# A windowed-attention transformer on one core: the scores split in two halves with a turn and a projection between them, and the output product moved to another PSUM bank

## The chip, the cores and the metric

One core of one Trainium2 chip runs the whole program. The time is the device time of one execution in microseconds (us). A kernel's figure is the median of several executions. Smaller is better.

## The reference, cut to what matters

The input x is 4 sequences of 512 tokens with 128 channels. First comes one RWKV time-mixing layer, then a transformer of 6 layers. This is the part of a layer that the change touches:

```python
def attn_layer(x, Wqkv, qs, ksc, Wo):          # x: (4, 512, 128), tokens shifted before
    q, k, v = split(x @ Wqkv, 3)               # 16 heads of 64
    q, k = l2norm(q) * qs, l2norm(k) * ksc     # then rotary tables on both
    ...
    # windows of 32 tokens; each looks at itself and the window before
    sim  = einsum('bhwie,bhwje->bhwij', bq, bk2) * 8.0
    sim  = where(mask, -max, sim)
    attn = softmax(sim, -1)
    out  = einsum('bhwij,bhwje->bhwie', attn, bv2)
    return out @ Wo                            # + x
# behind it: centre, normalise, x @ W1 + b1, a * gelu(gate), @ W2 + b2, + x
```

## The kernel before, in words

The function `time_mixing` does the RWKV layer in about the first 120 us of the profile. All that follows is `transformer`. Its work is cut into items, one for each layer and sequence (6 x 4 = 24), and each item into four blocks of 128 tokens, numbered t = 0 to 3. That makes 96 blocks. One step of the main loop handles several blocks at different ages: it projects block `step`, scores block `step - 2` and finishes block `step - 3`. Each engine has a program of its own written out by hand, in which the order of the calls is the order of execution. An engine waits only at a semaphore, and everything queued behind the waiting instruction waits with it.

In one step PE (TensorE) does the following, in this order (L1380 to L1415):

- `project` V0, Q0 and Q1: each is three matmuls of 128x512 (L1202 to L1204) into bank 0 or bank 1. Between them stand `turn_qk` of chunk 0 and, by t, the feed-forward pieces `expand` j=2 (t=1) and `centre` (t=3).
- at t=0, `widen_rstd` (L1341), which waits for `rooted`, the end of DVE's reciprocal square root (L922).
- `weigh(step-3, 1)`: the second half of probabilities times v, 64 small matmuls (L1284) into the two banks of the tensor `wide`. Of each bank's 512 columns, the first 4 x 65 = 260 are used.
- `turn_o(step-3, 0)`: four transposes (L1299) into bank 2. They wait for `o_normed`.
- `score(step-2)`: two mask matmuls (L1236), then 64 calls of small matmuls into banks 4 and 5. The trace counts each call as two matmuls and two weight loads (L1246 x12288 over 96 blocks, so 128 of each a block). Only the last call for each bank raises `scored`.
- `turn_o(step-3, 1)`, `project` K0, `project` K1, `turn_qk(step-1, 3)`.
- `merge_heads(step-3)`: the output product, 16 matmuls (L1313) into bank 4, columns 0 to 127. Since bank 4 also holds the scores, it waits until DVE's first `shift` has read them (`shifted[0]`).
- at t=1 `contract` (L1368), then `turn_probs` for r=0 and r=1 (L1264), each waiting for the exponential of its half. Then by t: `expand` j=0 (t=0), `turn_out` (t=2, last layer only), `variance` (t=3, L1332).
- `project` V1, which waits for `squared[2]`, then `turn_qk(step-1, 2)`, `weigh(step-2, 0)`, `turn_qk(step-1, 1)`, and at t=0 `expand` j=1, which waits for `hidden_ready`, DVE's gate (L984).

DVE (VectorE), in its order (L998 to L1027): `root`, `rotate` 0 (L879, L885), `normalise(step-3, 1)` (L946, L949), `rotate` 1, `maximum` 0 and 1 (L928, both wait for `scored`), `shift` 0 (L936), `sum_squares` 0 (L895), `shift` 1, `rotate` 2, `residual` (L959, reads the output product), `sum_squares` 1, `rotate` 3, and then `sum_squares` 2 and 3 and `normalise(step-2, 0)`, with `scale_xn`, `gate`, `take_var` and `finish_item` put in by t.

ACT (ScalarE), in its order (L1143 to L1178): `take_v`, `take_qk` 0 and 1, `square` 0 (L1064), `take_o` 0, `square` 1, `take_o` 1, `exponentiate` 0 (L1080), `take_qk` 3, `exponentiate` 1, at t=0 `shift_tokens`, `square` 2, `take_probs` 0 and 1 (L1087), at t=0 `gelu` (L1129), `square` 3, `take_qk` 2, `take_v` 1.

POOL (GpSimd) adds and normalises q and k (L795, L803). SP issues the DMAs.

Of the kernel before, what the change touches and what calls it, by code (L numbers as in the profile page):

```python
# [27 lines left out]
P = 128  # L28
BATCH, SEQ = 4, 512
DEPTH, HEADS, DH, WINDOW = 6, 16, 64, 32  # L30
INNER = HEADS * DH
NBLK = SEQ // P
NWIN = P // WINDOW
ITEMS = DEPTH * BATCH
BLOCKS = ITEMS * NBLK
# [47 lines left out]
def need(eng, sem, value, most=None):  # L83

    value = value if most is None else min(value, most)
    if value > 0:
        eng.wait_ge(sem, value)
# [531 lines left out]
def transformer(nc, bank, wide, weights, w_qkv, w_o, w_1, w_2, ident, center, mean_col, x_state, vecs, qk_rows,  # L619
# [12 lines left out]
    with ExitStack() as ctx:  # L632
# [17 lines left out]
        q_t = sb("q_t", [P, PAIRS, P])  # L650
        k_t = sb("k_t", [P, PAIRS, PAD + SEQ])
# [6 lines left out]
        o_t = sb("o_t", [P, 2, PAIRS, P])  # L658

        w_o_s = sb("w_o_s", [P, 2, PAIRS, P])  # L660
        w_1_s, w_2_s = sb("w_1_s", [P, 2 * DIM_INNER]), sb("w_2_s", [P, NHID, P])
        x1, xs2, hidden = sb("x1", [P, 2, SEQ]), sb("xs2", [P, SEQ]), sb("hidden", [P, NHID, SEQ])
# [10 lines left out]
        projected, qk_turned, scored, p_turned = sems("projected", 6), sems("qk_turned", 4), sem("scored"), sems("p_turned", 2)  # L673
# [5 lines left out]
        maxed, shifted, inverted, o_normed = sems("maxed", 2), sems("shifted", 2), sems("inverted", 2), sems("o_normed", 2)  # L679
        x1_done, var_taken, xn_scaled = sem("x1_done"), sem("var_taken"), sem("xn_scaled")  # L680
# [11 lines left out]
        def live(g):  # L692
            return 0 <= g < BLOCKS
# [10 lines left out]
        def batch_slot(item):  # L704
            return x_state[:, item % BATCH, :]

        def root_count(g):
            return g + 1 if live(g) else BLOCKS + 1

        def bank_of(c):  # L710
            return bank[c % 2]

# [145 lines left out]
        def _(dve):  # L858
# [94 lines left out]
            def residual(g):  # L953
                if not live(g):
                    return
                item, t = divmod(g, NBLK)
                cols = slice(P * t, P * (t + 1))
                dve.wait_ge(wo_done, g + 1)
                dve.tensor_tensor(x1[:, item % 2, cols], bank[4][:, 0:P], batch_slot(item)[:, cols],  # L959
                                  ALU.add).then_inc(x1_done, 1)  # L960

            def take_var(m):
# [218 lines left out]
        def _(pe):  # L1181
# [31 lines left out]
                                      qk[:, g % 2, c, j * P:(j + 1) * P], ident[:])  # L1213
                mm.then_inc(qk_turned[c], 1)

            def score(g, step):
                if not live(g):
                    return
                item, t = divmod(step, NBLK)
                for c in range(QK_CHUNKS):  # L1220
                    pe.wait_ge(qk_taken[c], g + 1)
                need(pe, x1_done, g - 1)
                need(pe, shifted[0], g)
                need(pe, shifted[1], g)
                if t == 0:
                    need(pe, xn_scaled, item - 1, ITEMS)
                if t == 1:
                    need(pe, hidden_ready, NHID * (item - 1), NHID * ITEMS)
                if t == 2:
                    need(pe, x2_done, item - 1, ITEMS)  # L1230
                if t == 3:
                    need(pe, cen_taken, 2 * item, 2 * ITEMS)
                if t == 0:
                    need(pe, var_taken, item - 1, ITEMS)
                for r in range(2):
                    pe.matmul(bank[4 + r][:], ident_bf[:], mask_bf[:, min(g % NBLK, 1), :], start=True, stop=True)  # L1236
                tok = P * (g % NBLK)
                for s in range(2):
                    for place in range(NWIN):
                        w = 2 * (place % 2) + place // 2  # L1240
                        col = (NWIN * s + place) * 2 * WINDOW
                        for h in range(4):
                            pair = 4 * s + h
                            for r in range(2):
                                row = slice(DH * r, DH * (r + 1))
                                mm = pe.matmul(bank[4 + r][WINDOW * h:WINDOW * (h + 1), col:col + 2 * WINDOW],  # L1246
                                               q_t[row, pair, WINDOW * w:WINDOW * (w + 1)],
                                               k_t[row, pair, tok + WINDOW * w:tok + WINDOW * w + 2 * WINDOW],
                                               start=False, stop=True, skip_group_check=True)
                                if s == 1 and place == NWIN - 1 and h == 3:  # L1250
                                    mm.then_inc(scored, 1)

            def turn_probs(g, r):
                if not live(g):
# [12 lines left out]
            def weigh(g, m):  # L1267
                if not live(g):
                    return
                item, t = divmod(g, NBLK)  # L1270
                if m == 0:
                    pe.wait_ge(p_taken[0], g + 1)
                    pe.wait_ge(p_taken[1], g + 1)
                    pe.wait_ge(v_moved[t], (16 if t == 0 else 32) * (item + 1))
                    need(pe, o_normed[1], g)
                else:
                    pe.wait_ge(o_normed[0], g + 1)
                for s in range(2):
                    for r in range(2):
                        quad = 2 * s + r  # L1280
                        for h in range(4):
                            for w in range(2):
                                row = slice(2 * WINDOW * w, 2 * WINDOW * (w + 1))
                                mm = pe.matmul(wide[WINDOW * h:WINDOW * (h + 1), w, quad * (DH + 1):(quad + 1) * (DH + 1)],  # L1284
                                               p_t[row, r, 2 * s + m, WINDOW * h:WINDOW * (h + 1)],
                                               v[row, t, m, 8 * s + 2 * h + r, :], start=True, stop=True)
                                if quad == 3 and h == 3:
                                    mm.then_inc(weighed[m], 1)
# [14 lines left out]
            def merge_heads(g):  # L1303
                if not live(g):
                    return
                layer = layer_of(g // NBLK)
                pe.wait_ge(w_o_loaded, 16 * (layer + 1))
                pe.wait_ge(o_taken[0], g + 1)
                pe.wait_ge(o_taken[1], g + 1)
                need(pe, shifted[0], g + 2, BLOCKS)  # L1310
                need(pe, x1_done, g)
                for p in range(PAIRS):
                    mm = pe.matmul(bank[4][:, 0:P], w_o_s[:, layer % 2, p, :], o_t[:, g % 2, p, :],  # L1313
                                   start=(p == 0), stop=(p == PAIRS - 1))
                mm.then_inc(wo_done, 1)

# [9 lines left out]
            def variance(m):  # L1326
                if not real(m):
                    return
                pe.wait_ge(cen_taken, 2 * (m + 1))
                need(pe, x1_done, NBLK * (m + 1) + 1, BLOCKS)  # L1330
                for j in range(NBLK):
                    mm = pe.matmul(bank[4][:, j:j + 1], xsq[:, j * P:(j + 1) * P], mean_col[:], start=True, stop=True)  # L1332
                mm.then_inc(var_done, 1)
# [46 lines left out]
            for step in range(STEPS):  # L1380
                item, t = divmod(step, NBLK)
                project(step, V0)
                project(step, Q0)
                turn_qk(step - 2, 0, qk_taken[2], step - 1)
                if t == 1:
                    expand(item - 2, 2)
                if t == 3:
                    centre(item - 1)
                project(step, Q1)
                if t == 0:  # L1390
                    widen_rstd(item - 2)
                weigh(step - 3, 1)
                turn_o(step - 3, 0)
                score(step - 2, step)
                turn_o(step - 3, 1)
                project(step, K0)
                project(step, K1)
                turn_qk(step - 1, 3, o_taken[1], step - 2)
                merge_heads(step - 3)
                if t == 1:  # L1400
                    contract(item - 2)
                turn_probs(step - 2, 0)
                turn_probs(step - 2, 1)
                if t == 0:
                    expand(item - 2, 0)
                if t == 2:
                    turn_out(item - 2)
                if t == 3:
                    variance(item - 1)
                project(step, V1)  # L1410
                turn_qk(step - 1, 2, p_taken[0], step - 1)
                weigh(step - 2, 0)
                turn_qk(step - 1, 1, p_taken[1], step - 1)
                if t == 0:
                    expand(item - 2, 1)  # L1415
# [26 lines left out]
```

## Time and profile before

| | us |
|---|---|
| median of 3 runs | 1769.03 (1767.48 to 1780.83) |
| the profiled execution | 1768.05 |
| its span, first to last instruction | 1766.3 |
| one step with t=1 (914.90 to 932.87) | 17.97 |
| one step with t=2 (932.87 to 946.80) | 13.93 |

The profile describes the one profiled execution. Its span leaves out 1.75 us that lie around it. PE rows are matmuls, PEld rows are their weight loads; the two overlap. A matmul's end is modelled, so the time from one PE start to the next start says more than a row's own duration. "Idle before" is the time in which the engine did nothing before that row, and "issue" means that it waited for nothing that the profile shows. Over the whole span TensorE was granted 0.970 of its full clock, and 1.00 in the steps from 881 to 962 us.

### The profile page before, as it was taken

How to read it: one execution, taken by the hardware profiler on the slowest of the kernel's cores; microseconds unless marked ns; L12 is line 12 of the kernel's file. 1: busy time of each engine (PE TensorE's matmuls, PEld its weight loads, DVE VectorE, ACT ScalarE, POOL GpSimd, SP SyncE). 2: the span in 40 equal slices, each digit the busy share in tenths (PEclk: the TensorE clock that was granted, in tenths of full speed). 3: DMA queues.
4: the chain of work that ended last, by engine and by line, in shares of the span. 5: the costliest groups of instructions: out<-in, count | busy, mean ns of one | idle time of the engine just before them, and what ended most of it. 6: DMA issues, size and time to landing. Idle time of an engine off the chain costs nothing.

```text
span 1766.3 us, 75410 instructions
## 1 busy us (share of the span) xinstructions
PE 1612.7 (91%) x31917; PEld 1243.7 (70%) x32013; DVE 1445.9 (82%) x3189; ACT 1106.9 (63%) x1990; POOL 998.8 (57%) x956
## 2 busy tenths in 40 slices
PE   5369998999899999999999999999999999999985
PEld 2137776777777777777778777777777777777763
DVE  8769887888788888888888888888888888878861
ACT  5236666667566666666766766666766666766652
POOL 2246655665556566556576567476467476465530
PEclk8579999999999999999999999999999999999997
DMA  3011101111111111201111111111111111011010
GB/s 103 26 52 37 51 24 48 45 42 36 51 36 39 48 35 39 60 24 51 48 36 40 39 45 51 44 40 39 36 47 52 40 43 39 28 50 51 24 45 13
DMA packets 40597, 74.95 MB, mean 42 GB/s; under 512 B 8992, under 2 KB 22088, under 8 KB 40264
## 3 DMA queue, kind: packets, MB, share of 16 engines
q1 hardware_dynamic: 40264, 70.11, 13.6%
q8 instruction: 257, 4.21, 1.0%
q14 instruction: 76, 0.62, 0.1%
HBM read 20.08 MB, written 2.10 MB: 13 GB/s over the span
## 4 chain that ended last, share of the span: by engine, by line
PE 82%; issue 5%; DVE 4%; POOL 2%; ACT 1%; DVEq 0%; POOLq 0%; ACTq 0%
PE bank L1212 9%; PE bank L1313 9%; PE wide L1284 8%; PE bank L1246 8%; PE bank L1202 7%; PE bank L1204 7%; PE bank L1203 7%; PE bank L1299 6%; PE bank L1264 4%; PE bank L1357 4%; PE bank L1358 4%; PE bank L1368 4%; PE bank L1236 2%; PE bank L1324 1%; PE bank L1332 1%
## 5 line engine op out<-in xcount | busy, mean ns | idle before, releaser
L795 POOL TENSOR_TENSOR qk<-qk,qk_sin 128x512 f32<-128x512 f32 x384 | 492.2, 1282 | 215.4 <-DVE qk_sin L885 215.4
L803 POOL TENSOR_TENSOR qk<-qk,rnorm 128x512 f32<-128x512 f32 x384 | 401.8, 1047 | 352.9 <-DVE rnorm L922 352.9
L1064 ACT ACTIVATE squares<-bank 128x512 f32<-128x512 f32 x384 | 229.1, 597 | 159.1 <-DVE qk_sin L885 157.3
L1202 PE MATMUL bank<-w_hi,xs_hi 128*128 128x512 f32 x576 | 290.4, 504 | 12.9 <-ACT squares L1064 6.9
L895 DVE TENSOR_REDUCE norm<-squares 128x8 f32<-128x512 f32 x384 | 258.3, 678 | 31.1 <-ACT squares L1064 28.9
L879 DVE TENSOR_TENSOR qk<-bank,tables 128x512 f32<-128x512 f32 x384 | 261.5, 681 | 6.4 <-PE bank L1204 5.4
L885 DVE TENSOR_TENSOR qk_sin<-bank,tables 128x512 f32<-128x512 f32 x384 | 261.0, 680 | 0.0
L1212 PE MATMUL bank<-ident,qk 128*128 128x128 f32 x1536 | 237.2, 278 | 2.6 <-POOL qk L803 1.8
L1204 PE MATMUL bank<-w_hi,xs_lo 128*128 128x512 f32 x576 | 230.3, 400 | 0.0
L1203 PE MATMUL bank<-w_lo,xs_hi 128*128 128x512 f32 x576 | 228.1, 396 | 0.0
L1212 PEld LDWEIGHTS bank<-ident,qk 128*128 128x128 f32 x1536 | 185.5, 142 | 51.2 <-issue 3.2
L1246 PEld LDWEIGHTS bank<-k_t,q_t 64*32 64x32 f32 x12288 | 131.3, 105 | 96.7 <-issue 96.2
L928 DVE TENSOR_REDUCE row_max<-bank 128x8 f32<-128x512 f32 x192 | 123.6, 686 | 91.9 <-PE bank L1246 91.7
L1246 PE MATMUL bank<-k_t,q_t 64*32 64x64 f32 x12288 | 154.7, 226 | 47.8 <-issue 47.4
L1313 PE MATMUL bank<-o_t,w_o_s 128*128 128x128 f32 x1536 | 193.3, 280 | 2.9 <-DVE probs L936 1.8
L1095 ACT COPY o_t<-bank 128x512 f32<-128x512 f32 x192 | 112.2, 584 | 123.2 <-PE bank L1299 123.0
L1313 PEld LDWEIGHTS bank<-o_t,w_o_s 128*128 128x128 f32 x1536 | 181.1, 194 | 5.4 <-issue 4.1
L1284 PEld LDWEIGHTS wide<-v,p_t 64*32 64x32 f32 x12288 | 134.4, 106 | 50.1 <-issue 47.9
L1284 PE MATMUL wide<-v,p_t 64*32 64x65 f32 x12288 | 166.1, 225 | 2.8 <-DVE o L949 1.1
L1080 ACT ACTIVATE probs<-probs 128x512 f32<-128x512 f32 x192 | 121.0, 631 | 63.6 <-DVE probs L936 57.5
L1202 PEld LDWEIGHTS bank<-w_hi,xs_hi 128*128 128x128 f32 x576 | 110.2, 191 | 52.8 <-issue 27.8
L1056 ACT COPY v<-bank 128x512 f32<-128x512 f32 x192 | 113.8, 592 | 49.4 <-PE bank L1204 48.9
(161 smaller groups left out, 2563.2 us busy)
## 6 DMA issues: line engine op xcount, KB each, us to landing
v<-v SPq DMA_DIRECT2D x96, 390.0 KB, 3.5
v<-v SPq DMA_DIRECT2D x72, 130.0 KB, 3.6
w_raw<-in_L_ffn_Wqkv SPq DMA_DIRECT2D x36, 256.0 KB, 3.7
w_o_s<-in_L_ffn_Wo SPq DMA_DIRECT2D x6, 512.0 KB, 5.0
w_s<-in_L_ffn_W SPq DMA_DIRECT2D x6, 341.0 KB, 5.0
mix_x_nat<-in_L_attn_x SPq DMA_DIRECT2D x4, 256.0 KB, 3.4
x_res_scratch<-mix_x_res SPq DMA_DIRECT2D x4, 256.0 KB, 2.8
w_raw<-x_res_scratch SPq DMA_DIRECT2D x4, 256.0 KB, 4.5
```

The lines of the kernel that those rows point to most:

```text
L795: pool.tensor_tensor(qk[:, g % 2, c, :], qk[:, g % 2, c, :], qk_sin[:, c, :], ALU.add).then_inc(added[c], 1)
L803: pool.tensor_tensor(view, view, rnorm[:, g % 2, c * HPC:(c + 1) * HPC].unsqueeze(2) .to_broadcast([P, HPC, DH]), ALU.mult).then_inc(norme ...
L879: dve.tensor_tensor(qk[:, g % 2, c, :].rearrange("p (h d) -> p h d", d=DH), src[:].rearrange("p (h d) -> p h d", d=DH), table(kind).unsque ...
L885: dve.tensor_tensor(qk_sin[:, c, :].rearrange("p (h a d) -> p h a d", a=2, d=DH // 2), src[:].rearrange("p (h a d) -> p h a d", a=2, d=DH ...
L895: dve.tensor_reduce(norm2[:, c * HPC:(c + 1) * HPC], squares[:, c % 2, :].rearrange("p (h d) -> p h d", d=DH), AX.X, ALU.add).then_inc(sum ...
L1202: pe.matmul(bank_of(c)[:], l_hi, w_hi[:, n, :], start=True, stop=False)
L1203: pe.matmul(bank_of(c)[:], l_hi, w_lo[:, n, :], start=False, stop=False)
L1204: pe.matmul(bank_of(c)[:], l_lo, w_hi[:, n, :], start=False, stop=True).then_inc(projected[c], 1)
L1212: mm = pe.transpose(bank[2 + c % 2][:, j * P:(j + 1) * P], qk[:, g % 2, c, j * P:(j + 1) * P], ident[:])
L1246: mm = pe.matmul(bank[4 + r][WINDOW * h:WINDOW * (h + 1), col:col + 2 * WINDOW], q_t[row, pair, WINDOW * w:WINDOW * (w + 1)], k_t[row, pai ...
L1284: mm = pe.matmul(wide[WINDOW * h:WINDOW * (h + 1), w, quad * (DH + 1):(quad + 1) * (DH + 1)], p_t[row, r, 2 * s + m, WINDOW * h:WINDOW * ( ...
L1313: mm = pe.matmul(bank[4][:, 0:P], w_o_s[:, layer % 2, p, :], o_t[:, g % 2, p, :], start=(p == 0), stop=(p == PAIRS - 1))
```

## The change

The scores of a block are done in two calls. `open_scores` has the waits and the two mask matmuls, `score(g, s)` has the 32 calls of one half. The first half stays where the whole was. Behind it come `turn_o(step-3, 1)` and `project` K0, and only then the second half, and `project` K1. `scored` is still raised at the end of the second half alone.

The output product no longer goes to bank 4 but to columns 260 to 387 of the first bank of `wide`, beside the outputs of the weighing. DVE's `residual` reads it there. With that `merge_heads` no longer waits for `shifted[0]` or `x1_done`; it waits for `o_normed[1]` of its own block. `weigh(g, 0)` gets a wait for `x1_done` of the block before, the scores lose theirs, and `variance` waits for `shifted[0]` where it waited for `x1_done`.

```diff
--- before.py
+++ after.py
@@ -707,6 +707,8 @@
         def root_count(g):
             return g + 1 if live(g) else BLOCKS + 1
 
+        merged = wide[:, 0, 4 * (DH + 1):4 * (DH + 1) + P]
+
         def bank_of(c):
             return bank[c % 2]
 
@@ -956,7 +958,7 @@
                 item, t = divmod(g, NBLK)
                 cols = slice(P * t, P * (t + 1))
                 dve.wait_ge(wo_done, g + 1)
-                dve.tensor_tensor(x1[:, item % 2, cols], bank[4][:, 0:P], batch_slot(item)[:, cols],
+                dve.tensor_tensor(x1[:, item % 2, cols], merged, batch_slot(item)[:, cols],
                                   ALU.add).then_inc(x1_done, 1)
 
             def take_var(m):
@@ -1213,13 +1215,12 @@
                                       qk[:, g % 2, c, j * P:(j + 1) * P], ident[:])
                 mm.then_inc(qk_turned[c], 1)
 
-            def score(g, step):
+            def open_scores(g, step):
                 if not live(g):
                     return
                 item, t = divmod(step, NBLK)
                 for c in range(QK_CHUNKS):
                     pe.wait_ge(qk_taken[c], g + 1)
-                need(pe, x1_done, g - 1)
                 need(pe, shifted[0], g)
                 need(pe, shifted[1], g)
                 if t == 0:
@@ -1234,21 +1235,25 @@
                     need(pe, var_taken, item - 1, ITEMS)
                 for r in range(2):
                     pe.matmul(bank[4 + r][:], ident_bf[:], mask_bf[:, min(g % NBLK, 1), :], start=True, stop=True)
+
+            def score(g, s):
+
+                if not live(g):
+                    return
                 tok = P * (g % NBLK)
-                for s in range(2):
-                    for place in range(NWIN):
-                        w = 2 * (place % 2) + place // 2
-                        col = (NWIN * s + place) * 2 * WINDOW
-                        for h in range(4):
-                            pair = 4 * s + h
-                            for r in range(2):
-                                row = slice(DH * r, DH * (r + 1))
-                                mm = pe.matmul(bank[4 + r][WINDOW * h:WINDOW * (h + 1), col:col + 2 * WINDOW],
-                                               q_t[row, pair, WINDOW * w:WINDOW * (w + 1)],
-                                               k_t[row, pair, tok + WINDOW * w:tok + WINDOW * w + 2 * WINDOW],
-                                               start=False, stop=True, skip_group_check=True)
-                                if s == 1 and place == NWIN - 1 and h == 3:
-                                    mm.then_inc(scored, 1)
+                for place in range(NWIN):
+                    w = 2 * (place % 2) + place // 2
+                    col = (NWIN * s + place) * 2 * WINDOW
+                    for h in range(4):
+                        pair = 4 * s + h
+                        for r in range(2):
+                            row = slice(DH * r, DH * (r + 1))
+                            mm = pe.matmul(bank[4 + r][WINDOW * h:WINDOW * (h + 1), col:col + 2 * WINDOW],
+                                           q_t[row, pair, WINDOW * w:WINDOW * (w + 1)],
+                                           k_t[row, pair, tok + WINDOW * w:tok + WINDOW * w + 2 * WINDOW],
+                                           start=False, stop=True, skip_group_check=True)
+                            if s == 1 and place == NWIN - 1 and h == 3:
+                                mm.then_inc(scored, 1)
 
             def turn_probs(g, r):
                 if not live(g):
@@ -1273,6 +1278,7 @@
                     pe.wait_ge(p_taken[1], g + 1)
                     pe.wait_ge(v_moved[t], (16 if t == 0 else 32) * (item + 1))
                     need(pe, o_normed[1], g)
+                    need(pe, x1_done, g)
                 else:
                     pe.wait_ge(o_normed[0], g + 1)
                 for s in range(2):
@@ -1307,10 +1313,9 @@
                 pe.wait_ge(w_o_loaded, 16 * (layer + 1))
                 pe.wait_ge(o_taken[0], g + 1)
                 pe.wait_ge(o_taken[1], g + 1)
-                need(pe, shifted[0], g + 2, BLOCKS)
-                need(pe, x1_done, g)
+                pe.wait_ge(o_normed[1], g + 1)
                 for p in range(PAIRS):
-                    mm = pe.matmul(bank[4][:, 0:P], w_o_s[:, layer % 2, p, :], o_t[:, g % 2, p, :],
+                    mm = pe.matmul(merged, w_o_s[:, layer % 2, p, :], o_t[:, g % 2, p, :],
                                    start=(p == 0), stop=(p == PAIRS - 1))
                 mm.then_inc(wo_done, 1)
 
@@ -1327,7 +1332,7 @@
                 if not real(m):
                     return
                 pe.wait_ge(cen_taken, 2 * (m + 1))
-                need(pe, x1_done, NBLK * (m + 1) + 1, BLOCKS)
+                need(pe, shifted[0], NBLK * (m + 1) + 2, BLOCKS)
                 for j in range(NBLK):
                     mm = pe.matmul(bank[4][:, j:j + 1], xsq[:, j * P:(j + 1) * P], mean_col[:], start=True, stop=True)
                 mm.then_inc(var_done, 1)
@@ -1391,9 +1396,11 @@
                     widen_rstd(item - 2)
                 weigh(step - 3, 1)
                 turn_o(step - 3, 0)
-                score(step - 2, step)
+                open_scores(step - 2, step)
+                score(step - 2, 0)
                 turn_o(step - 3, 1)
                 project(step, K0)
+                score(step - 2, 1)
                 project(step, K1)
                 turn_qk(step - 1, 3, o_taken[1], step - 2)
                 merge_heads(step - 3)
```

## Rows read from the trace of the kernel before

**Rows 1.** The page, section 1: busy time, share of the span, instructions of each engine.
```profile
PE 1612.7 (91%) x31917; PEld 1243.7 (70%) x32013; DVE 1445.9 (82%) x3189; ACT 1106.9 (63%) x1990; POOL 998.8 (57%) x956
```

**Rows 2.** The waits, whole span: waiter, releaser, us in total, times, longest us.
```profile
PEld bank L1246 <- issue: 96.2, 143, 3.2
PE bank L1246 <- issue: 47.4, 40, 3.1
PEld bank L1202 <- ACT squares L1064: 9.9, 26, 2.5
PEld bank L1341 <- DVE rnorm L922: 16.5, 24, 2.2
PEld bank L1357 <- DVE hidden L984: 8.2, 24, 2.1
```

**Rows 3.** The page, section 3: a DMA queue, its kind, packets, MB, share.
```profile
q8 instruction: 257, 4.21, 1.0%
```

**Rows 4.** Timeline of PEld, scores of a step with t=0: start, us, idle before.
```profile
899.62 1.20 PEld L1246 LDWEIGHTS bank<-k_t,q_t 64*32 64x32 f32 x115 [0.42 <-issue]
901.85 0.17 PEld L1246 LDWEIGHTS bank<-k_t,q_t 64*32 64x32 f32 x13 [1.03 <-issue]
```

**Rows 5.** Timeline of PE in the next step, t=1, from the scores on.
```profile
919.46 1.48 PE L1246 MATMUL bank<-k_t,q_t 64*32 64x64 f32 x128
920.88 0.66 PE L1299 MATMUL bank<-ident,o 128*128 128x128 f32 x4
...
925.01 2.74 PE L1368 MATMUL bank<-hidden,w_s 128*128 128x512 f32 x6
927.60 1.04 PE L1264 MATMUL bank<-ident,probs 128*128 128x128 f32 x8
```

**Rows 6.** Timeline of PE in the step after it, t=2, from Q1 to V1.
```profile
933.04 0.39 PE L1203 MATMUL bank<-w_lo,xs_hi 128*128 128x512 f32 x1
933.27 0.40 PE L1204 MATMUL bank<-w_hi,xs_lo 128*128 128x512 f32 x1
933.60 0.86 PE L1284 MATMUL wide<-v,p_t 64*32 64x65 f32 x64
...
937.08 0.66 PE L1299 MATMUL bank<-ident,o 128*128 128x128 f32 x4
937.49 0.48 PE L1202 MATMUL bank<-w_hi,xs_hi 128*128 128x512 f32 x1
...
938.27 0.39 PE L1202 MATMUL bank<-w_hi,xs_hi 128*128 128x512 f32 x1
...
941.21 1.04 PE L1264 MATMUL bank<-ident,probs 128*128 128x128 f32 x8
...
942.17 0.50 PE L1202 MATMUL bank<-w_hi,xs_hi 128*128 128x512 f32 x1
```

**Rows 7.** Timeline of DVE and ACT in the same step, t=2, behind the scores.
```profile
937.21 1.29 DVE L928 TENSOR_REDUCE row_max<-bank 128x8 f32<-128x512 f32 x2 [0.55 <-PE bank L1246]
...
940.32 0.63 ACT L1080 ACTIVATE probs<-probs 128x512 f32<-128x512 f32 x1
...
941.52 0.60 ACT L1064 ACTIVATE squares<-bank 128x512 f32<-128x512 f32 x1 [0.56 <-DVE qk_sin L885]
```

**Rows 8.** Timeline of ACT, DVE and PEld, t=0, from the second exponential on.
```profile
905.41 0.63 ACT L1080 ACTIVATE probs<-probs 128x512 f32<-128x512 f32 x1
...
910.70 0.75 DVE L984 SCALAR_TENSOR_TENSOR hidden<-bank,vecs,xsq_gated 128x512 f32<-128x512 f32 x1 [2.12 <-ACT xsq_gated L1129]
...
911.50 0.30 PEld L1357 LDWEIGHTS bank<-xc_xn,w_s 128*128 128x128 f32 x2 [0.19 <-DVE hidden L984]
```

**Rows 9.** Timeline of DVE and PEld from the end of t=3 into t=0.
```profile
960.31 0.21 DVE L946 RECIPROCAL row_sum<-wide 128x8 f32<-128x8 f32 x1 [0.29 <-PE wide L1284]
...
963.21 0.41 PEld L1341 LDWEIGHTS bank<-ident,rnorm 128*128 128x128 f32 x4 [0.28 <-DVE rnorm L922]
```

**Rows 10.** Timeline of DVE at the end of t=1.
```profile
929.84 0.69 DVE L895 TENSOR_REDUCE norm<-squares 128x8 f32<-128x512 f32 x1 [1.29 <-ACT squares L1064]
```

## The prediction

> **What bounds the kernel now.** I read the busy shares first, then the waits, then three consecutive steps (t = 0, 1, 2) and the seam from t=3 to t=0 as a timeline, engine by engine. The busy shares show PE at 91% and DVE at 82% [rows 1], so PE is the resource. The waits show that PE stands still for two sorts of reason [rows 2]. One is "issue": 47.4 us in 40 gaps inside the score matmuls, and 96.2 us on the weight-load side. The other sort is small in sum, but it marks three places where PE already runs without slack. V1 waits for a square 26 times, the widening of rstd waits for the root 24 times, and `expand` waits for the gate 24 times; 24 is the number of items, so two of these come once in each item.
>
> The issue gaps first. A block's scores are 128 weight loads and 128 matmuls. In the step of [rows 4], 115 of the loads pass in 1.20 us, about 0.010 us each; then they stop and go on 1.03 us later. Undisturbed, all 128 pairs and the way out to the next turn take 919.46 to 920.88 = 1.42 us [rows 5]. Queue q8 brought 257 packets of instructions, 4.21 MB, 16.4 KB each [rows 3]. PE and PEld together ran 63,930 instructions [rows 1], or 249 for each packet. So I read the gap as PE outrunning its instruction supply: 256 instructions of scores pass in some 1.3 us, and nothing else in the step is that dense for that long. How large is it in all? The load side shows 96.2 us, of which each block's ordinary entry into the scores is 0.42 [rows 4]. 96 x 0.42 = 40, and 96.2 - 40 = 56 us.
>
> Next, the way the end of the scores sets the step. At t=2 the last score matmul starts about 0.15 us before the turn at 937.08. DVE takes the maxima at 937.21, having waited 0.55 us for exactly that. It works without a pause through both shifts and K0's rotation, so that ACT's square starts at 941.52 and ends at 942.12. V1 starts at 942.17 [rows 6, 7]. From the end of the scores to V1 a chain of DVE and ACT work of about 5.1 us runs beside PE work that is just as long. Any PE work moved from behind the scores to before their end makes this chain stick out.
>
> **The change, part by part.**
>
> *The split takes cover away.* The second half, and with it `scored`, comes after `turn_o` 1 and K0. On PE these take 937.08 to 937.49 = 0.41 and 937.49 to 938.27 = 0.78 [rows 6]. So 1.19 us of PE work that lay beside the DVE chain now lies ahead of it.
>
> *It adds two changes of tile shape.* Going from a full-size matmul to small ones costs 933.27 to 933.60 = 0.33, where two full-size ones stand 0.23 apart [rows 6]: 0.10 more. Leaving the small ones costs 1.42 - 128 x 0.010 = 0.14, rounded to 0.15 [rows 4, 5]. Together 0.25 us a step, always on PE. Bounds: 0.0, if both pipeline away, and 0.42, if each entry costs as much as the entry to the scores [rows 4]. I take 0.25, as these rows are the same kinds of edge.
>
> Now each kind of step, with the end of the scores 1.19 + 0.25 = 1.44 us later than before:
>
> - t=1: `contract` stands between the merge and the turned probabilities, 925.01 to 927.60 = 2.59 us [rows 5]. It covers 1.19. Later DVE waits 1.29 us for ACT's square, which hangs on PE's turned probabilities [rows 10], so nothing is carried into t=2. Cost 0.25.
> - t=2: nothing stands between `turn_probs` and V1. V1 stays 5.1 us behind the end of the scores [rows 6, 7]. Cost 1.44.
> - t=0: ACT runs from the second exponential (905.41) nearly without a pause through the token shift, a square, two copies, a table load and the gelu. DVE's gate waits 2.12 us for it, and `expand` waits for the gate [rows 8]. This chain too starts at the end of the scores. Cost 1.44.
> - t=3: the second exponential ends 940.95 in the t=2 step, and the second half of `turn_probs` starts at about 941.21 + 0.44 = 941.65 [rows 6, 7], a slack of 0.70. I take the same here. So PE waits 1.19 - 0.70 = 0.49 there, and `variance` behind it covers the square. But DVE stays late and goes on into the root. Its only pause on the way is 0.29 us [rows 9], and the widening at t=0 starts the moment the root is ready. All in all 1.44 - 0.29 = 1.15.
>
> Sum of an item: 0.25 + 1.44 + 1.44 + 1.15 = 4.28 us, and 24 items make 103 us. With the shape changes at 0.0 it is 79 us, at 0.42 it is 119 us.
>
> *The split gives back instruction gaps.* The gaps lie late in the scores, and the block of 256 instructions that runs out there began before or early in them. With 1.44 us of sparse work in its middle, a gap of up to 1.44 vanishes. The 40 gaps on PE have a mean of 1.2 us and a longest of 3.1 [rows 2], so I let 6 of the 56 us stay. Gain 50 us. Bounds: 0, if the gaps aren't of this kind, and 56.
>
> The Trainium skill ("Runtime: NRT & Kernel Launch", section "Instruction fetch mechanics") says that an engine's instructions come in 16 KiB blocks of 256, and the packets' size agrees [rows 3]. It also gives PE room for 2048 instructions and calls the cost of a block boundary mostly hidden; the gap of 1.03 us [rows 4] speaks against "hidden" here. By the page nothing is gained from thinning the burst, which is the third rival below.
>
> *The merge in another bank.* `merge_heads` no longer waits for the first shift. Before, PE hardly waited there, so nothing is gained. It is what keeps the loss at 1.19: with the old wait the merge would now be held too. The new waits cost nothing. `o_normed[1]` was already waited for by `turn_o` 1, and the residual (DVE, right behind K0's rotation) is done well over 1 us before `weigh` 0. I allow 0 to 5 us either way for bank sharing, and take 0. The other changed waits are of the same order of age; DMAs and the queues of SP and POOL are not moved.
>
> *Sum:* 1768.05 + 103 - 50 = 1821 us. The profiled execution is 1 us under the median of the runs, so the median should come out the same, about 1821 us, +3%.
>
> **The rivals.**
>
> 1. *The gaps are worth more than the lateness (faster).* If the DVE and ACT chain has more play than three steps show, the split costs only its shape changes, 24 x 4 x 0.25 = 24 us, and the fetch gain of 50 us wins: 1768 - 26 = 1742. For it: 56 us of gaps is the largest idle of PE. Against it: V1, the widening and `expand` wait in about every item [rows 2], which leaves no play. It decides in its favour only if less than 50 of the 103 us appear, that is, if two of the three chained steps an item hide their 1.19.
> 2. *Both cancel (no change).* With the shape changes at 0.0 and all 56 us of gaps gone, 1768 + 79 - 56 = 1791. Another 10 us or more of cover (say, DVE catching up over the layer seams) would bring it under 1786.
> 3. *The gaps stay (the page's rule).* The lateness is paid in full and nothing comes back: 1768 + 103 = 1871. For it: I see the packets only as a sum. Against it: a stop of 1.03 us in the middle of identical matmuls, without a semaphore, is hard to explain otherwise.
>
> **How the numbers follow.** Forecast as above: 0.70. Rival 1: 0.09. Rival 2: 0.11. Rival 3: 0.10. The forecast's own range is 1790 to 1845, from the bounds of the shape changes (79 to 119) and a gain of 40 to 56. To leave out no more than 2 in 10 I go down to 1775 and up to 1850. What a measurement of this kernel can tell from no change is about 1% (18 us): slower by more than that holds the forecast, rival 3 and a little of rival 2, 0.81; within 1% 0.10; faster 0.09.
>
> **What would show each step right or wrong.** Right, if the "issue" idle of PE at the score line falls from 47.4 to under 10 us; if the waits of PE or PEld for squares (V1), for the exponentials (`turn_probs`), for the root and for the gate rise by some 80 us together; if DVE's wait for the score line grows by about 1.4 us a step; and if the step with t=1 grows least and t=2 and t=0 most. K0 to the second half should show the 0.33 of an entry, and the way out 0.15. Wrong, if V1 at t=2 follows the end of the scores in much less than 5.1 us, if the gaps stay in the second half (rival 3), or if the end of the scores moves by less than 1.2 us against the work ahead of it.

## The result, and the profile after

The changed kernel took 1827.2 us in the median of 4 runs (1821.1 to 1828.95), the kernel before 1772.2 in the same sets. The ratio is 1.0292, 95% interval 1.0258 to 1.0326: slower, as forecast. The quotient of the two medians alone would be 1.031. The profiled execution took 1827.9 us against 1768.05 before, 59.9 us more, where the forecast had 53.

The busy shares of the changed kernel (columns as in [rows 1]):

```profile
span 1826.0 us, 75342 instructions
...
PE 1666.4 (91%) x31917; PEld 1237.8 (68%) x32013; DVE 1442.0 (79%) x3189; ACT 1097.0 (60%) x1990; POOL 998.4 (55%) x956
...
PE 56%; DVE 19%; issue 13%; ACT 7%; DVEq 0%; ACTq 0%; POOL 0%
```

The last line is the chain of work that ended last. Before it was:

```profile
PE 82%; issue 5%; DVE 4%; POOL 2%; ACT 1%; DVEq 0%; POOLq 0%; ACTq 0%
```

PE's busy share is still 91%, and by it nothing has happened. The chain tells more. PE's part of it fell from 82% to 56%; DVE and ACT together went from 5% to 26%, and "issue" from 5% to 13%. PE has stopped being the only bound.

The waits of the changed kernel (waiter, releaser, us in total, times, longest), to be read against [rows 2]:

```profile
DVE row_max L930 <- PE bank L1251: 182.6, 96, 4.0
...
PEld bank L1251 <- issue: 88.1, 212, 2.2
...
PEld bank L1269 <- ACT probs L1082: 41.4, 74, 1.6
...
PEld bank L1204 <- ACT squares L1066: 24.1, 30, 2.5
...
PEld bank L1346 <- DVE rnorm L924: 22.3, 24, 2.4
...
PEld bank L1362 <- DVE hidden L986: 13.0, 26, 2.5
...
PE bank L1251 <- issue: 9.3, 12, 2.0
```

Two things moved, and in opposite directions. The issue gaps of PE in the scores fell from 47.4 us in 40 gaps to 9.3 in 12. The waits for other engines rose: squares from 9.9 to 24.1, the root from 16.5 to 22.3, the gate from 8.2 to 13.0. The wait for the exponentials is new: 41.4 us in 74 of the 96 steps, against 1.7 us in 2 before. DVE stands 1.9 us a step before its maxima (182.6 / 96), where it was 1.0 before (91.7 us in 92). The rows of before for these two are:

```profile
DVE row_max L928 <- PE bank L1246: 91.7, 92, 3.9
...
PEld bank L1264 <- ACT probs L1080: 1.7, 2, 0.9
```

The forecast had named both sizes. The four waits of PEld together rose from 36.3 to 100.8 us, 64.5 more, where it had some 80. DVE's wait grew by 0.95 us a step, where it had about 1.4. The scores do end 1.44 us later, but the gaps that vanished inside them (some 44 us, 0.46 a step, worked out below) make DVE's wait shorter again.

The timeline of PE in a step with t=2 of the changed kernel, against [rows 6]:

```profile
895.11 0.86 PE L1251 MATMUL bank<-k_t,q_t 64*32 64x64 f32 x64
895.90 0.66 PE L1305 MATMUL bank<-ident,o 128*128 128x128 f32 x4
896.31 0.48 PE L1204 MATMUL bank<-w_hi,xs_hi 128*128 128x512 f32 x1
...
897.18 0.86 PE L1251 MATMUL bank<-k_t,q_t 64*32 64x64 f32 x64
897.97 0.50 PE L1204 MATMUL bank<-w_hi,xs_hi 128*128 128x512 f32 x1
...
900.99 0.60 PE L1269 MATMUL bank<-ident,probs 128*128 128x128 f32 x4
901.90 0.66 PE L1269 MATMUL bank<-ident,probs 128*128 128x128 f32 x4 [0.30 <-ACT probs L1082]
903.06 0.50 PE L1204 MATMUL bank<-w_hi,xs_hi 128*128 128x512 f32 x1 [0.51 <-ACT squares L1066]
```

And DVE and ACT in the same step, against [rows 7]:

```profile
898.10 1.29 DVE L930 TENSOR_REDUCE row_max<-bank 128x8 f32<-128x512 f32 x2 [1.72 <-PE bank L1251]
...
901.22 0.63 ACT L1082 ACTIVATE probs<-probs 128x512 f32<-128x512 f32 x1
902.41 0.60 ACT L1066 ACTIVATE squares<-bank 128x512 f32<-128x512 f32 x1 [0.57 <-DVE qk_sin L887]
```

From the maxima to V1 it is 903.06 - 898.10 = 4.96 us, exactly as before (942.17 - 937.21 = 4.96). In this step the chain has not changed by a hundredth. It only begins later, measured against the PE work, because a part of that work now stands ahead of it. So the second half of the turned probabilities waits for the exponential, and V1 waits again for the square.

### The profile page after: what moved, and what is told of

The parts are those of the page before. It is cut to its first block, busy times and chain, and to the rows that moved or that the text cites. A ratio compares the mean times of both kernels' runs of the same rounds, so it can differ in the third digit from the quotient of the medians.

```text
span 1826.0 us, 75342 instructions
## 1 busy us (share of the span) xinstructions
PE 1666.4 (91%) x31917; PEld 1237.8 (68%) x32013; DVE 1442.0 (79%) x3189; ACT 1097.0 (60%) x1990; POOL 998.4 (55%) x956
## 4 chain that ended last, share of the span: by engine, by line
PE 56%; DVE 19%; issue 13%; ACT 7%; DVEq 0%; ACTq 0%; POOL 0%
PE bank L1251 9%; PE wide L1290 6%; PE bank L1305 6%; DVE norm L897 5%; PE bank L1204 5%; PE bank L1206 5%; PE bank L1214 5%; PE bank L1205 5%; DVE probs L938 4%; PE bank L1373 4%; PE bank L1362 3%; DVE qk_sin L887 3%; PE bank L1363 2%; PE bank L1237 2%; ACT squares L1066 2%
## 5 line engine op out<-in xcount | busy, mean ns | idle before, releaser
L1204 PE MATMUL bank<-w_hi,xs_hi 128*128 128x512 f32 x576 | 299.9, 521 | 25.0 <-ACT squares L1066 18.8
L930 DVE TENSOR_REDUCE row_max<-bank 128x8 f32<-128x512 f32 x192 | 123.7, 687 | 182.6 <-PE bank L1251 182.6
L1251 PEld LDWEIGHTS bank<-k_t,q_t 64*32 64x32 f32 x12288 | 135.9, 105 | 88.7 <-issue 88.1
L1318 PE MATMUL wide<-o_t,w_o_s 128*128 128x128 f32 x1536 | 189.6, 277 | 1.0 <-ACT o_t L1097 0.9
L1318 PEld LDWEIGHTS wide<-o_t,w_o_s 128*128 128x128 f32 x1536 | 181.3, 194 | 1.5 <-issue 1.5
L1251 PE MATMUL bank<-k_t,q_t 64*32 64x64 f32 x12288 | 170.9, 224 | 9.9 <-issue 9.3
L951 DVE TENSOR_TENSOR o<-wide,row_sum 128x512 f32<-128x512 f32 x192 | 132.8, 692 | 7.2 <-DVE row_sum L948 0.7
```

The costliest lines, as they stand in the source:

```text
L1204: pe.matmul(bank_of(c)[:], l_hi, w_hi[:, n, :], start=True, stop=False)
L1318: mm = pe.matmul(merged, w_o_s[:, layer % 2, p, :], o_t[:, g % 2, p, :], start=(p == 0), stop=(p == PAIRS - 1))
```

## The experiments

In all runs "gaps" is PE's idle time by "issue" at the score line, in us, from each kernel's waits. The "undisturbed step" is worked out from the trace: from one V0 to the next, less the time by which the step's scores took longer than undisturbed. The scores are measured from the end of their first weight load to the end of their last matmul. Undisturbed, that is 1.38 us (in one piece), 2.13 (a turn between) or 2.82 (turn and K0 between). Steps are given as medians over steps 8 to 91. Each run has its own ratio to the kernel before, taken in the same sets; times of different runs in us are good to some 5 us, as the kernel before itself had medians of 1772 to 1778 in the four sets.

The theory under test: the loss is the work put ahead of the end of the scores (lateness, 1.19 us) and the changes of shape, less the instruction gaps that the thinner burst gives back. Its rivals: the split as such costs it, wherever things stand; the bank move costs it; the gaps have nothing to do with the burst.

**1. The bank move alone.**

```diff
                 turn_o(step - 3, 0)
                 open_scores(step - 2, step)
                 score(step - 2, 0)
+                score(step - 2, 1)
                 turn_o(step - 3, 1)
                 project(step, K0)
-                score(step - 2, 1)
                 project(step, K1)
```

> The output product in the wide bank with its changed waits, the scores in one piece again. Lateness theory (all of the loss comes from the 1.19 us of work put ahead of the end of the scores and from the shape changes): no split, no loss, ratio to before 0.995 to 1.005, issue gaps of PE at the score line back at 45 to 60 us, no exponential waited for at the turned probabilities. Rival (sharing a bank with the weighing, or the new wait of the weighing for the residual, costs time): ratio 1.01 or more, with waits in front of the output product or the weighing.

Measured: ratio 0.9986 (0.9966 to 1.0006), gaps 44.6, and 1.6 us of waits for the exponentials. No loss. Neither the shared bank nor the new waits cost anything that can be measured, and the removed wait gives nothing by itself.

**2. The split alone**, with the product in bank 4 and the waits of before.

```diff
-        merged = wide[:, 0, 4 * (DH + 1):4 * (DH + 1) + P]
+        merged = bank[4][:, 0:P]
...
-                pe.wait_ge(o_normed[1], g + 1)
+                need(pe, shifted[0], g + 2, BLOCKS)
+                need(pe, x1_done, g)
```

> The split alone: the output product goes to bank 4 again and waits for the first shift. Lateness theory: the product now waits for a shift that ends 2.06 us behind the scores, while PE is there at 1.28, so it is held 0.8 us; at t=1 this reaches the contraction (0.6 us an item), at t=3 perhaps 0.3, at t=2 and t=0 nothing, as the square and the gate end later anyway. Some 15 to 25 us above the changed kernel, 1840 to 1852 us, ratio to before 1.037 to 1.046. Rival (the bank move costs something of its own, the split less than the whole): at or below the changed kernel, ratio 1.03 or less.

Measured: ratio 1.0448 (1.0416 to 1.0480), 1855.4 us, the upper end of what was expected. Its waits:

```profile
PE bank L1319 <- DVE probs L938: 86.2, 95, 2.2
```

The output product (L1319 here) waits for the first shift in 95 blocks, 0.91 us each. PEld's later waits are back near their size of before: 2.4 us for the exponentials, 9.0 for squares, 8.3 for the gate, 16.3 for the root. The product's wait stands in their place, which is why 86 us of it cost only some 28 more. So the two edits belong together: the bank move is worth nothing without the split (run 1), and some 28 us with it (1855.4 - 1827.2; by the two ratios 0.0156 x 1772, also 28).

**3. Only the turn between the halves**, K0 and K1 behind both.

```diff
                 score(step - 2, 0)
                 turn_o(step - 3, 1)
+                score(step - 2, 1)
                 project(step, K0)
-                score(step - 2, 1)
                 project(step, K1)
```

> Only the turn stands between the halves, K0 is behind both again. Lateness theory: 0.41 us late in place of 1.19, 0.27 of shape changes. t=1 0.27, t=2 and t=0 0.66 to 0.7 each, t=3 with the widening 0.4, together 2.0 us an item or 48 us, less a third to a half of the gaps (0.66 us of thinning, 25 to 32 us): 1768 + 18 = 1786, ratio 1.006 to 1.016. Issue gaps left at the score line about half of before's. Rival (the cost is the splitting as such, two halves with changes of shape, whatever stands between): as slow as the changed kernel, 1.025 or more.

Measured: ratio 1.0069 (1.0041 to 1.0097), gaps 24.3. Inside the range. With 0.41 us of lateness in place of 1.19, three quarters of the loss are gone, while the scores are cut in two just the same. The split as such isn't the cause of most of it.

**4. The early turn between the halves**: nothing is put ahead of the end of the scores.

```diff
-                turn_o(step - 3, 0)
                 open_scores(step - 2, step)
                 score(step - 2, 0)
+                turn_o(step - 3, 0)
+                score(step - 2, 1)
                 turn_o(step - 3, 1)
                 project(step, K0)
-                score(step - 2, 1)
                 project(step, K1)
```

> Between the halves stands the turn that stood ahead of both, so nothing is put ahead of the end of the scores, but the same two changes of shape are there and the burst is thinned by 0.66 us. Lateness theory: 4 x 0.25 x 24 = 24 to 30 us of shape changes, less 25 to 32 us of gaps: ratio 0.995 to 1.005, no new wait for exponentials or squares. Rival (the splitting as such): 1.025 or more. Rival for the gaps (they do not come from the density of the burst): gaps stay at 45 us or more on PE and the ratio is 1.013 or more.

Measured: ratio 1.0083 (1.0052 to 1.0115), gaps 31.3; outside the range, upwards. There was no new wait for exponentials (1.6 us) or squares (9.6), so the lateness is gone as expected. Two sizes were off. The undisturbed step grew by 0.31 to 0.35 us at t=1, 2 and 3, where I had 0.25 for the shape changes, and by 0.78 at t=0. There the first score follows the start of the weighing at the same 2.0 us as before, although the turn has left that place. The mask matmuls in front of it wait for DVE's scaled activations:

```profile
PE bank L1237 <- DVE xc_xn L976: 18.7, 23, 0.9
```

That is 0.81 us in nearly every step with t=0. So the turn had been free there and now costs its 0.41. And the gaps gave back less: 16 us (47.4 - 31.3) where 25 to 32 were expected.

**5. K0 ahead of the scores**, the scores in one piece, no change of shape added.

```diff
                 turn_o(step - 3, 0)
+                project(step, K0)
                 open_scores(step - 2, step)
                 score(step - 2, 0)
+                score(step - 2, 1)
                 turn_o(step - 3, 1)
-                project(step, K0)
-                score(step - 2, 1)
                 project(step, K1)
```

> The scores in one piece, the output product in the wide bank, and K0 moved ahead of the scores, so that the end of the scores is 0.78 us late without any change of shape and without any thinning inside the scores. Lateness theory: t=2 and t=0 0.78 each, t=3 with the widening 0.5, t=1 up to 0.1, and at t=0 K0 may wait some tenths for its square; 2.1 to 2.6 us an item, 50 to 62 us; the gaps stay (PE 45 to 60 us at the score line). 1820 to 1830 us, ratio 1.028 to 1.036. Rival (the loss is the splitting): ratio 1.01 or less. Rival for the gaps (any work moved there fills them): gaps fall by half or more.

Measured: ratio 1.0268 (1.0234 to 1.0302), just under the expected range. Nearly the whole loss of the change comes back without any split. But two expectations failed. K0 waited more for its square than I had thought, and the gaps fell by more than half, as the rival for the gaps had it, although nothing thinned the scores themselves:

```profile
PE bank L1204 <- ACT squares L1066: 50.7, 78, 2.1
...
PE bank L1251 <- issue: 20.3, 24, 2.2
```

By its place in the step, K0 has 38.1 of these 50.7 us: 1.15 in each step with t=0 and 0.33 in each with t=2. This wait too stands ahead of the end of the scores, so their end is later by more than K0's own 0.78. Run 5 therefore shows that a loss of this size needs no split; it does not show what 0.78 us of lateness costs by itself.

**6. The changed kernel with DVE and ACT put in the order that the split allows.** DVE rotates K0 before the maxima, in its 1.9 idle us, and ACT squares it before the exponentials.

```diff
# DVE
+                sum_squares(step, 0)
+                rotate(step, 2)
                 maximum(step - 2, 0)
                 maximum(step - 2, 1)
                 shift(step - 2, 0)
-                sum_squares(step, 0)
                 shift(step - 2, 1)
-                rotate(step, 2)
# ACT
+                square(step, 2)
+                take_qk(step - 1, 3)
                 exponentiate(step - 2, 0)
-                take_qk(step - 1, 3)
                 exponentiate(step - 2, 1)
...
-                square(step, 2)
                 take_probs(step - 2, 0)
# PE, ahead of turn_qk(step - 1, 1); bank 3 is read by take_qk 3
+                if live(step - 1):
+                    need(pe, qk_taken[3], step)
```

> The changed kernel with DVE and ACT put in the order that the split allows: DVE sums the first squares and rotates K0 before the maxima, in the 1.9 us a step in which it waits for the scores, and does both shifts in a row; ACT squares K0 and copies the keys before the exponentials. Lateness theory: the chain from the end of the scores to V1 and to the turned probabilities is 0.5 us and more shorter, nothing of it sticks out, and what stays is 0.25 to 0.36 us of shape changes a step (24 to 35 us) against 45 us of gaps recovered and some old waits gone: 1740 to 1762 us, ratio 0.983 to 0.997. Rival (the lateness isn't what costs, PE's own work has grown): at most a third of the loss returns, ratio 1.02 or more.

Measured: ratio 0.9927 (0.9900 to 0.9954), 1763.9 us. The PE program is the changed kernel's but for one wait, and 63 us are gone (65 by the two ratios). Its DVE in a step with t=2:

```profile
933.75 0.68 DVE L897 TENSOR_REDUCE norm<-squares 128x8 f32<-128x512 f32 x1
934.73 0.69 DVE L881 TENSOR_TENSOR qk<-bank,tables 128x512 f32<-128x512 f32 x1 [0.31 <-PE bank L1206]
935.34 0.68 DVE L887 TENSOR_TENSOR qk_sin<-bank,tables 128x512 f32<-128x512 f32 x1
935.94 1.28 DVE L930 TENSOR_REDUCE row_max<-bank 128x8 f32<-128x512 f32 x2
937.13 1.28 DVE L938 TENSOR_TENSOR probs<-bank,row_max 128x512 f32<-128x512 f32 x2
```

and its waits:

```profile
PEld bank L1269 <- ACT probs L1082: 15.9, 76, 2.0
...
DVE row_max L930 <- PE bank L1251: 10.8, 9, 2.2
...
PE bank L1251 <- issue: 9.7, 13, 1.9
```

K0's rotation sits in the former hole before the maxima, DVE's wait for the scores fell from 182.6 to 10.8 us, and the gaps are as small as in the changed kernel. The chain is shorter, as expected: at t=2 V1 follows the maxima after 3.60 us (median), where it was 4.96. With the lateness out of the way, what is left is the gaps given back against the changes of shape. One rival stands: the new order was not run on the kernel before, with the scores in one piece and K0 behind them. So it isn't shown that the 0.7% needs the split, only that the split no longer costs anything.

**7. K0 ahead of the scores, with the same new order** (run 5 and run 6 together).

> K0 ahead of scores in one piece, with the same new order of DVE and ACT. Lateness theory: DVE has only about 1.1 us before the end of the scores for 1.9 us of work, so the maxima start about 0.8 us late, and the second exponential is ready some tenths after PE reaches it; 0 to 0.4 us a step for three of four steps, and the gaps of 45 to 60 us stay: 1768 to 1795 us, ratio 1.000 to 1.015, better than K0 ahead without the new order by 25 us or more and worse than the split with the new order by 20 us or more. Rival (the gaps cost nothing, or the split gives nothing back): as good as or better than the split with the new order.

Measured: ratio 1.0138 (1.0096 to 1.0179), 1801.7 us: 25 us better than run 5 and 38 worse than run 6, a little above the expected 1795. The gaps were expected to stay at 45 to 60 us and did not. Two of its waits:

```profile
PE bank L1204 <- ACT squares L1066: 40.9, 57, 1.4
...
PE bank L1251 <- issue: 24.2, 27, 1.9
```

K0 has 38.2 of the 40.9 us (2.0 in run 6), which by itself is as much as the distance to run 6; the gaps are 14.5 us larger than there. So in runs 5 and 7 K0, which waits for the square of Q0, stands too close behind it, and that is a cost of its own.

**8. Only Q1 moved**, in the kernel before, to test the gaps by themselves.

```diff
-                project(step, Q1)
+                weigh(step - 3, 1)
                 if t == 0:
                     widen_rstd(item - 2)
-                weigh(step - 3, 1)
+                project(step, Q1)
                 turn_o(step - 3, 0)
```

> The kernel before with one move on PE: Q1 stands behind the second weighing, next to the turn and the masks, and no longer ahead of it (at t=0 the order is weighing, widening, Q1). The scores stay in one piece and in their place, so nothing is late and no change of shape is added. Supply theory (a gap is the time by which a block of 256 instructions is run through faster than the next one arrives; K0 ahead of the scores cut the gaps from 60 to 27 us this way): the 0.7 us of Q1 now lie in nearly every block that ends in the scores, the gaps fall by 25 to 33 us (PE's at the score line from 47 to 20 to 25), 1735 to 1750 us, ratio 0.981 to 0.990. Rival (the gaps shrank in the other runs because PE waited more or the scores were cut, not because of the work in front): ratio 0.995 to 1.005, PE gaps 40 us or more. Rival (Q1 later delays DVE's rotation and with it the maxima): ratio above 1.0, DVE waits less for the scores and V1 more for its square.

Measured: ratio 0.9904 (0.9883 to 0.9925), 1762.1 us, gaps 37.8. It is faster, but the ratio is a hair above the expected range and the time 12 us above it. The gaps shrank by 10 us, not 25; that lies nearer to the rival (40 us or more) than to the theory. Part of the gain is elsewhere: PEld waits 8.1 us for the root at the widening, where it was 16.5. So 0.7 us of work in front of the scores filled the gaps less well than 0.66 us between the halves did (47.4 to 24.3 in run 3, to 31.3 in run 4). Run 5 had 0.78 us of K0 in front and on top of it K0's wait, which I had left out when I carried its gaps over to this run. That this explains the difference is argued, not shown.

**9. Run 6 with the same move of Q1.**

> The split with the new order of DVE and ACT, and the same move of Q1. Supply theory: only some 15 us of gaps are left in the split kernel, mostly in the first half and behind late fetches, so the move gives 5 to 10 us there: ratio 0.986 to 0.992, no better than the unsplit kernel with Q1 moved. Rival (the two gains add up in full, 13 and 25 us): ratio 0.978 or less.

Measured: ratio 0.9915 (0.9898 to 0.9932), gaps 3.9, both inside what was expected. The gains don't add up. Runs 6, 8 and 9 are all faster than both kernels, and their intervals overlap.

## Why the prediction was right, point by point

The undisturbed steps, and what the forecast gave to each:

| step | before | changed | more | forecast |
|---|---|---|---|---|
| t=1 | 17.98 | 18.71 | 0.73 | 0.25 |
| t=2 | 13.55 | 14.98 | 1.44 | 1.44 |
| t=3 | 15.12 | 15.96 | 0.84 | } 2.59 |
| t=0 | 17.41 | 19.01 | 1.60 | } for both |
| an item | 64.06 | 68.66 | 4.60 | 4.28 |

- *The split takes cover away, 1.19 us.* Right. The undisturbed scores from first to last went from 1.38 to 2.82 us, 1.44 more, which is 1.19 and the 0.25. Runs 3 and 4 keep the split and take lateness away, and most of the loss goes; run 6 keeps both and shortens the chain that the lateness lays bare, and all of it goes.
- *Shape changes, 0.25.* The entry (0.33) and the way out (897.18 to 897.97 = 0.79, of which 0.64 are the pairs) came as said. But K1, now behind scores, takes 1.24 us to the output product (897.97 to 899.21) in place of 1.13 before. It is 0.36 on PE, and 0.31 to 0.35 in run 4.
- *t=2, 1.44.* Right: the scores end that much later, and V1 stays 4.96 us behind the maxima. That it is right to the hundredth is luck, as the changes of shape in it were rounded to 0.05.
- *t=1, covered by the contraction, 0.25.* This is the step that failed: it measured 0.73, the largest miss of the four. The contraction writes bank 5, which holds scores, so it waits for the second shift:

```profile
951.41 1.95 PE L1318 MATMUL wide<-o_t,w_o_s 128*128 128x128 f32 x16
953.53 2.81 PE L1373 MATMUL bank<-hidden,w_s 128*128 128x512 f32 x6 [0.17 <-DVE probs L938]
```

  It starts 2.12 us after the product began (953.53 - 951.41), where it was 1.82 before (median). That is 0.30 us that I did not see, as I had read its cover but not its wait. The wait shows in 22 of the 24 items:

```profile
PE bank L1373 <- DVE probs L938: 4.5, 22, 0.6
```

  In runs 3 and 4, with less lateness, it is gone: the contraction follows the product after 1.79 us. With the 0.36 of shape changes and 0.07 by which the way from the contraction to the turned probabilities grew (2.58 to 2.65), this makes the 0.73.
- *t=0 and t=3, 2.59 together.* 2.44. The widening waits, the gate waits and the exponentials wait where it was said. At t=3 the forecast had PE waiting 0.49 us for the exponential, and its second half of turned probabilities starts 0.47 later than before (0.91 behind the first half in place of 0.44). The forecast divided the sum as 1.15 and 1.44, the trace as 0.84 and 1.60, so their sum is nearer than either. Their places show in a chain of small waits: 0.56 us for the exponential, then 0.36 for the gate, in one step with t=0 (PEld):

```profile
933.95 0.42 PEld L1269 LDWEIGHTS bank<-ident,probs 128*128 128x128 f32 x4 [0.56 <-ACT probs L1082]
...
939.36 0.30 PEld L1362 LDWEIGHTS bank<-xc_xn,w_s 128*128 128x128 f32 x2 [0.36 <-DVE hidden L986]
```

- *Gaps, 50 of 56 us given back.* By the length of the scores over their undisturbed length, they sum up to some 60 us before and 16 after: 44 back.
- *Sum.* 4.60 x 24 = 110 us, less 44, is 66; with means over the steps in place of medians (4.4 an item) it is 62, against 59.9 measured. The forecast was 103 - 50 = 53. Its two misses, on the loss and on the gaps, both lie to the slow side and are small; inside the loss, what was missed at t=1 (0.48 an item) was in part made up by what was put too high at t=3 and t=0 (0.15).
- *The rivals.* That the gaps outweigh the lateness fell: there was no hidden play in the chain. Run 6 shows what that rival would have needed, a DVE and ACT order that makes the play. That both cancel fell with it. That the gaps stay fell too: PE's gaps at the score line were 47.4 us before and 9.3 after with the same number of instructions. The Trainium skill ("Runtime: NRT & Kernel Launch", section "Instruction fetch mechanics") calls the cost of a block boundary mostly hidden. The 47.4 us do not agree with that, as far as the gaps are waits for a block (last section).

## What to carry to other kernels

When an engine's busy share is near full, a reordering costs what the other engines' chain loses in cover: find the instruction that starts the chain (here the last score), count the work that moves across it, and look for every wait behind it, also inside the work that you count as cover. A reorder on one engine is half a change: the same split went from 2.9% slower to 0.7% faster when the two engines that wait for it were reordered to use the hole. And look for "issue" gaps in the middle of a long run of identical small instructions. Here they were 47.4 us of PE's idle time, and what the packets say of them (next section) is that the run had outrun its own supply.

## What the runs showed of the hardware that was not expected

In five of these kernels (before, changed, runs 4, 5 and 8) I set the gaps over 0.3 us against the packets of the instruction queue. The median gap ended 2.36 to 2.44 us after the start of the last packet ahead of it, and 1.35 to 1.44 us after its end, whatever stood around the scores. The spread is small: in all of this case's kernels every such gap ended between 1.19 and 1.64 us after the end of a packet, although the packets themselves start some 6 us apart. That fits a wait for the next block of instructions. What makes a fetch start is not settled: the number of instructions between the fetch and the gap varied from under 50 to over 230, and moving 0.7 us of work in front of the burst (run 8) took back only 10 us of PE's 47. No run varied the block or the supply itself.
